# Transformer block with a second conditioned block: dense pieces placed otherwise over the steps of a turn, two score units taken a turn ahead

## The reference

```python
scale, shift = jnp.split(gelu(time_emb) @ Wt + bt, 2, axis=-1)
h = layer_norm(x, ln1_g, ln1_b) * (1.0 + scale[:, None, :]) + shift[:, None, :]
q, k, v = heads(h @ Wqkv)                       # 16 heads of 16
scores = einsum('bhqd,bhkd->bhqk', q, k) / 4 - torus_dist[:, None] * torus_scale[None, :, None, None]
scores = where(~mask[:, None, None, :], -1e30, scores)
x = x + merge(softmax(scores) @ v) @ Wout
h2 = layer_norm(x, ln2_g, ln2_b)
x = x + (gelu(h2 @ W1 + b1) @ W2 + b2)          # W1 256 x 1024
```

## Time and profile before

| | us |
|---|---|
| median of 3 runs | 1450.1 (1447.25 to 1451.61) |
| the profiled execution | 1447.55 |
| its span | 1445.7 |
| turn 0 | 85.8 |
| turns 1 to 7 | 107.3, 107.6, 107.6, 107.6, 108.7, 107.6, 107.9 |
| turns 8 to 15 with the end | 562.7 |

### The profile page before, as it was taken

The page is one execution under the profiler, slowest core; times in us unless marked ns, Lnnn a source line. Parts: engine busy times, 40 slices in busy tenths (PEclk is TensorE's granted clock), DMA queues, the critical chain, the costliest instruction groups (busy, mean ns, idle before and its releaser), DMA issues. The chain is left out here.

```text
span 1445.7 us, 24552 instructions
## 1 busy us (share of the span) xinstructions
PE 1310.9 (91%) x8789; PEld 1000.0 (69%) x8789; DVE 800.9 (55%) x2240; ACT 770.5 (53%) x1262; POOL 754.8 (52%) x939
## 2 busy tenths in 40 slices
PE   4898999999999999999999997889888888888887
PEld 3576777777777777777777776666666666665656
DVE  4766745746645645645644743474545646464452
ACT  3565764664665664665665662544545344454432
POOL 3788866876876875876876771020413223140323
PEclk9899999999999999999999999999999999999888
DMA  8432222222222222222223224443424242433100
GB/s 259 131 120 55 73 93 65 68 89 67 70 86 67 72 83 67 75 81 68 77 77 101 71 72 126 152 135 115 145 76 158 64 153 87 130 112 91 45 2 29
DMA packets 98259, 133.98 MB, mean 93 GB/s; under 512 B 16802, under 2 KB 51498, under 8 KB 98130
## 3 DMA queue, kind: packets, MB, share of 16 engines
q1 hardware_dynamic: 96850, 131.80, 30.4%
q10 hardware_dynamic: 1280, 0.53, 0.1%
HBM read 72.64 MB, written 58.75 MB: 91 GB/s over the span
## 5 line engine op out<-in xcount | busy, mean ns | idle before, releaser
L619 POOL TENSOR_SCALAR shifted<-shifted,row_max 128x512 f32<-128x512 f32 x512 | 358.9, 714 | 222.7 <-DVE row_max L1382 220.4
L1382 DVE CUSTOM_DVE_ANT_0 shifted<-score,bias 128x512 f32<-128x512 f32 x512 | 332.6, 687 | 255.9 <-PE score L857 163.6
L1093 ACT ACTIVATE probs<-turned 128x512 f32<-128x512 f32 x512 | 278.2, 596 | 211.5 <-PE turned L869 209.9
L869 PE MATMUL turned<-ident,shifted 128*128 128x128 f32 x2048 | 270.3, 275 | 6.8 <-POOL shifted L619 6.0
L869 PEld LDWEIGHTS turned<-ident,shifted 128*128 128x128 f32 x2048 | 233.8, 141 | 55.5 <-issue 26.4
L785 PE MATMUL dense<-w_down,hidden 128*128 128x256 f32 x1024 | 250.4, 381 | 0.8 <-ACT hidden L1074 0.8
L612 POOL TENSOR_SCALAR bias<-dist,scale 128x1024 f32<-128x1024 f32 x192 | 218.8, 1140 | 13.9 <-DMA down_bias<-in_L_cond_b 13.9
L857 PE MATMUL score<-k_rows,q_rows 97*128 97x512 f32 x512 | 205.1, 456 | 21.8 <-DVE row_max L1382 10.3
L785 PEld LDWEIGHTS dense<-w_down,hidden 128*128 128x128 f32 x1024 | 182.5, 190 | 32.5 <-issue 9.6
L765 PE MATMUL dense<-feat_m,w_up 128*128 128x512 f32 x768 | 188.9, 401 | 3.4 <-ACT hidden L1074 1.8
L765 PEld LDWEIGHTS dense<-feat_m,w_up 128*128 128x128 f32 x768 | 144.7, 192 | 37.2 <-ACT hidden L1074 5.2
(11 more groups left out here) (138 smaller groups left out, 1550.4 us busy)
## 6 DMA issues: line engine op xcount, KB each, us to landing
qk_rows<-qk_high SPq DMA_DIRECT2D x128, 256.0 KB
q_rows<-qk_rows SPq DMA_DIRECT2D x64, 384.0 KB
qk_rows<-qk_low SPq DMA_DIRECT2D x64, 256.0 KB
k_rows<-qk_rows SPq DMA_DIRECT2D x68, 192.0 KB
x_in_t<-in_x SPq DMA_DIRECT2D x8, 512.0 KB, 3.9
x_res<-in_x SPq DMA_DIRECT2D x8, 512.0 KB, 5.5
x_mid<-x_norm SPq DMA_DIRECT2D x8, 512.0 KB, 3.3
x_in_t<-x_mid SPq DMA_DIRECT2D x8, 512.0 KB, 3.9
```

The lines of the kernel that those rows point to most:

```text
L619: ins = pool.tensor_scalar(shifted[:, u % 3, i, :], shifted[:, u % 3, i, :], -1.0, row_max[:, t % 6:t % 6 + 1], ALU.mult, ALU.add)
L869: mm = pe.transpose(turned_bank[z % 2][:, HALF * kk + P * i:HALF * kk + P * i + P], shifted[:, u % 3, i, P * kt:P * kt + P], ident[:, :])
L1093: act.activation(probs[:, u % RING, 2 * pair:2 * pair + 2, :], turned_bank[z % 2][:, :].rearrange("p (a c) -> p a c", a=2), ACT.Exp)\
L1382: dve.tensor_tensor_reduce(shifted[:, u % 3, i, :], score_bank[t % 2], bias[:, u % 2, i, :], 1.0, 3.0e38, ALU.add, ALU.min, row_max[:, t % ...
```

## The change

The table `FIRST` puts the dense pieces elsewhere: `v` 2 and 3 a step apart at 3 and 4, `wout` 0 and 1 at 5 and 6 with `t1` behind them at 8 and 9, `qk` at 12, 13, 14 and 16 in place of 11 to 14, `up` two a step in steps 17, 18, 20 and 21 in place of four in 17 and four in 21, `down` from step 22 on in 14 parts in place of 11 from 25. The statistics and the normalization of the next input go from steps 2 and 4 to 4 and 6 (POOL's part from 2 to 4), the bias adds from 14 to 17 to 17, 18, 20 and 21. And the scores of units 0 and 1 of the next turn are taken by PE and DVE in steps 33 and 35 of this one (`AHEAD`), so that steps 0 and 1 of turns 1 to 7 hold none; turn 0 takes its own, turn 7 none ahead. POOL's and ACT's order for these units stays.

```diff
-    FIRST = {0: [("v", 0)], 1: [("v", 1)], 2: [("t3", 0), ("t3", 1)], 4: [("v", 2)], 5: [("v", 3), ("t1", 0)],
-             6: [("t1", 1)], 7: [("wout", 0)], 8: [("wout", 1)], 9: [("wout", 2)], 10: [("wout", 3)],
-             11: [("qk", 0)], 12: [("qk", 1)], 13: [("qk", 2)], 14: [("qk", 3)], 15: [("t2", 0), ("t2", 1)],
-             17: [("up", 0), ("up", 1), ("up", 2), ("up", 3)], 21: [("up", 4), ("up", 5), ("up", 6), ("up", 7)],
-             27: [("down", 0)], 30: [("down", 1)], 32: [("down", 2)], 35: [("down", 3)]}
+    FIRST = {0: [("v", 0)], 1: [("v", 1)], 2: [("t3", 0), ("t3", 1)], 3: [("v", 2)], 4: [("v", 3)],
+             5: [("wout", 0)], 6: [("wout", 1)], 8: [("t1", 0), ("wout", 2)], 9: [("t1", 1)], 10: [("wout", 3)],
+             12: [("qk", 0)], 13: [("qk", 1)], 14: [("qk", 2)], 15: [("t2", 0), ("t2", 1)],
+             16: [("qk", 3)], 17: [("up", 0), ("up", 1)], 18: [("up", 2), ("up", 3)], 20: [("up", 4), ("up", 5)],
+             21: [("up", 6), ("up", 7)],
+             25: [("down", 0)], 28: [("down", 1)], 31: [("down", 2)], 35: [("down", 3)]}
+
+    AHEAD = {33: 0, 35: 1}
     STEPS = UNITS + 5
-    FIRST_DOWN = {25: (0, 2), 26: (2, 5), 27: (5, 8), 28: (8, 12), 29: (12, 14), 30: (14, 17), 31: (17, 20),
-                  32: (20, 24), 33: (24, 26), 34: (26, 29), 35: (29, 32)}
-    FIRST_NORM = {2: ("stats", 0), 4: ("norm", 0), 11: ("stats", 1), 13: ("norm", 1)}
-    ADD_BIAS = {14: 0, 15: 1, 16: 2, 17: 3}
+    FIRST_DOWN = {22: (0, 2), 23: (2, 3), 24: (3, 6), 25: (6, 9), 26: (9, 12), 27: (12, 13), 28: (13, 16),
+                  29: (16, 19), 30: (19, 22), 31: (22, 24), 32: (24, 27), 33: (27, 28), 34: (28, 30), 35: (30, 32)}
+    FIRST_NORM = {4: ("stats", 0), 6: ("norm", 0), 11: ("stats", 1), 13: ("norm", 1)}
+    ADD_BIAS = {17: 0, 18: 1, 20: 2, 21: 3}
...
+    def begun(n, u):
+        return 0 < n < B and u in AHEAD.values()
...
-                        if k == 2 and n + 1 < B:
+                        if k == 4 and n + 1 < B:
                             inverse_std(n + 1, 0)
...
-                    if k < UNITS:
+                    if k < UNITS and not begun(n, k):
                         scores(n, k)
+                    if n + 1 < B and k in AHEAD:
+                        scores(n + 1, AHEAD[k])
...
-                    if k < UNITS:
+                    if k < UNITS and not begun(n, k):
                         shift_scores(n, k)
+                    if n + 1 < B and k in AHEAD:
+                        shift_scores(n + 1, AHEAD[k])
```

## The result

| | before | after |
|---|---|---|
| median of 4 runs each | 1448.67 (1446.25 to 1451.61) | 1426.82 (1425.15 to 1429.44) |
| profiled execution, its span | 1447.55, 1445.7 | 1427.12, 1425.3 |
| ahead of turn 0 | 43.5 (span less the rest) | 45.3 |
| turn 0 | 85.8 | 84.5 |
| turns 1 to 6 | 107.3, 107.6, 107.6, 107.6, 108.7, 107.6 | 104.4 each |

The account below looks back on a forecast made before the run. PE looks the bound, but waits drawn as busy lose 8.4 us a turn. Gains 1.2 + 1.5 + 0.2 - 0.4 = 2.5, taken as 2.3, times seven turns give 16 us: forecast 1433 us, range 1412 to 1450.

Parts of the forecast that it names:

- `qk` 3: Steps 15 to 17: moving it to step 16 gives ACT time to empty `t2`; 1.5 us a turn gained.
- the start: First `v` to step 8's pair: scores ahead cut lost time from 4.6 to 3.4 us, 1.2 gained.
- `up` two a step: Steps 17 to 22: 2.3 us of waits go, 2.1 paid back through ACT's table changes, 0.2 gained.
- `down` early: From step 22 in 14 parts: same products, five or six more changes of kind, -0.4 us a turn.
- the hand chain: Start of a turn, followed from the first `v`: shift 4 ends 9.1 us, shift 5 12.4.
- The wait named: Transposes after step 17's pair: 1.97 us later in place of 0.46, 1.5 lost, all of it to go.
- the gain of 2.3: Behind both blocks of `up` products: waits of 1.1 to 1.2 us a block go with two a step.
- Turn 0: First turn, without back work: what moves there cancels, 0 us, bounds -1 and +2.
- ACT as the bound: Rival, steps 17 to 22: added table changes cost PE 5.2 us; 1454 to 1462, decides from 4.4 lost; chance 0.12.
- the wait at unit 18: Transposes of unit 18 wait about 1.6 us for ACT's exps; forecast wrong if over 4 us.
- Nearly all waits go: Rival: start loses 1 us, not 3.4, and loads hide; 5 us and over a turn, 1405 to 1413; chance 0.12.
- Moved, not removed: Rival: normalization costs as much at step 6, ACT waits eat steps 15 to 17; 1444 to 1452; chance 0.14.

Follow-up runs that it names:

- experiment 3: The changed kernel with the next input's statistics and normalization back in steps 2 and 4: turn 105.67 us, median 1432.89, 0.9902 of before.
- experiment 4: The changed kernel with the four `qk` pieces back in steps 11 to 14, none in step 16: turn 105.06 us, median 1432.86, 0.9881 of before.
- experiment 8: The changed kernel with `down` back in 11 parts from step 25: turn 105.69 us, median 1430.43, 0.9882 of before.
- experiment 2: The kernel before with only the scores of two units taken ahead: most turns 106.55 us, median 1438.72, 0.9919 of before.

## Why the prediction was right, and where its steps were not

The sign, the place of the main waits and the total held: 1426.8 measured, 1433 forecast. That the total came within 0.9 us a turn is in part luck: of the four terms of the sum, `qk` 3 and `up` were put some 0.8 too high each, the start and `down` about 1.7 too low each by the single removals below, and these errors offset each other. What each part is worth to after, by taking it away alone, beside the forecast:

| part | forecast | taken away alone |
|---|---|---|
| scores ahead | together 1.2 | 1.64 (1.08 put in alone) |
| first norm at 6 | (in the 1.2) | 1.28 |
| `qk` 3 to step 16 | 1.5 | 0.67 |
| `up` two a step | 0.2 | -0.62 |
| `down` early, in 14 parts | -0.4 | 1.30 |
| bias adds | 0 | 0.0 |
| `v` 2 and 3 apart, `t1` and `wout` exchanged | (in the -0.4) | not run |
| sum | 2.5, taken as 2.3 | 4.27 |
| the turn | | 3.24 |

The parts do not add: taken away singly they make 1.0 more than together. Scores ahead are worth 1.08 without the rest and 1.64 with it. So part of the 1.0 lies between them and the rest, perhaps the norm, and some may lie between `up` and `down`; no run takes away just two of the parts.

**The start** (forecast 3.4 lost of 4.6). Right in kind: DVE is what the pairs wait for, and normalization in front of a shift costs a wait. A step that failed is the size of a pair of shifts: I took about 1.45, two lengths of 0.69 and a read each; by their starts they follow 0.61 apart, 1.22 to 1.3 a pair. In after shift 4 ends 8.55 us from the first `v` and shift 5 11.46, where the hand chain had 9.1 and 12.4; of the 0.9 by which it was late at shift 5 some 0.6 are the three pairs of shifts in it. Counted from start to start, pairs 4, 5, 6 and 8 lose 0.3, 0.4, 0.9 and 0.4, the transposes of unit 5 0.2, pair 11 0.5: 2.7. I also gave 1.1 to pair 8 behind the normalization, and it lost 0.4, because the attention of step 7 stands over it; experiment 3 shows what it costs without that cover. Pair 15 and the `qk` piece ahead of it, which lose 0.6 behind the second norm, I had not counted. Taken away alone, scores ahead and norm are worth 2.9 together, well over the 1.2 of the forecast; the singles overlap with other parts, so this is an upper mark.

**`qk` 3** (1.5). The wait named is gone, 0.53 in place of 1.97. The step that failed is the costing of the move as that alone: all four pieces shift, pair 15 then loses 0.5 behind the second norm and 0.3 is lost ahead of it, and experiment 4 shows 0.67 net.

**`up` two a step** (0.2). The payment was right in place and 0.6 too high: 2.1 forecast, 1.5 in the trace, 1.48 by taking the gelu away. The step that failed is the gain of 2.3. Nearly half of it (0.9 by the starts in before), the losses behind the second block, went through the early `down` products, whatever the grain of `up`. Against the 1.1 of the first block alone the change of grain loses. And the waits behind a block are not only DVE's and POOL's cold start, as the prediction had them: shift 19 stands idle 2.50 us in before for the bias that ACT makes late. The rule of the Trainium skill (ScalarE: Activation LUTs, Rules for kernel authors) to do all of one table set before switching is borne out here, by 0.62 us a turn. The drain that the same page adds to the load is not: ACT's rows have 1.29 from the start of a load to the gelu, and the next instruction of ACT starts within 0.02 of a load's end.

**`down` early** (-0.4). The step that failed outright: I counted it as the same products with more changes of kind, and it is the filler of steps 22 to 24, 1.30 won. The prediction said of this block that three pairs come close together, and did not ask what would then stand between them, nor that ACT's bias for unit 23 comes late there. It has POOL (2.2 a step) as what the steps must cover; in experiment 8 pair 24 waits behind ACT's bias.

**Turn 0** (0, bounds -1 and +2): 1.2 less by one profile of each, which shows no gain. Before without gelu has the same work in turn 0, and its profile gives 83.9 where that of before gives 85.8; the granted clock over it is 0.98 and 0.96.

**The rivals.** ACT as the bound: it is full from 489.4 to 500.5, but the wait at unit 18 is 1.0, far under the 4.4 from which that rival decides. Nearly all waits go: no, some 5 us a turn are left. Moved, not removed: true of the step from before's `up` waits to after's table waits, not of the turn. Of the marks that I set, the turn was to be 105 to 105.5 and is 104.4; the eight loads, POOL's 3.65 (under 5), the clean transposes of unit 15 and the 0.5 at the first `down` product are there; the wait at unit 18 is 1.0 and not 1.6. Pairs 5 to 8 with their transposes lose 1.9, inside the 1 to 5 that I set, and the first scores ahead wait for no load: the pair at 540.85 needs 0.66 to its successor, like those around it.

## What to carry to other kernels

A light step of the first engine lays bare whatever another engine is late with. Here the bias that ACT makes behind the gelus came 3.3 us late for DVE in both kernels, and cost PE nothing where `down` products stood in those steps; moving them there was worth 1.30 us a turn. So look for the steps where a helper is late, and put filler there. Put a long instruction of a queue that others wait for behind the longest piece of work that can cover it, and cost each piece that a move takes away from under another. Undo each part alone once a bundle has won: here one part of it lost, and leaving that out, with the norms, `t1`, `wout` and `qk` placed anew, brought 10 to 13 us more.

## What the runs showed of the hardware that was not expected

**A change of tables costs its load alone, and starts early.** In after the gelus of 490.71 end about 492.10, the load runs from 492.11 to 493.39 and the exps start at 493.41. Nor does the load wait for the operand of the ACTIVATE behind it: that at 489.42 began while PE, which had started the two `up` pieces at 488.36 (3.01 for both), could not have ended the first before about 489.8. The Trainium skill (ScalarE: Activation LUTs, What ACT_TABLE_LOAD costs) gives the same 1283 ns for the load; no row here shows the drain that it adds. A group of turn 4 of after:

```profile
L1083 ACT ACT_TABLE_LOAD x4 | 5.1, 1283 | 0.1
```

**The same DVE instruction takes half as long again beside POOL.** The second norm in before, with POOL idle for most of it, POOL first:

```profile
491.00 1.37 POOL L619 TENSOR_SCALAR shifted<-shifted,row_max 128x512 f32<-128x512 f32 x2 [2.32 <-DVE row_max L1382]
...
488.35 1.44 DVE L1222 TENSOR_SCALAR x_norm<-x_res,mean_var,rstd 128x256 f32<-128x256 f32 x4
```

and in after, with POOL at work through most of it:

```profile
475.18 1.12 POOL L619 TENSOR_SCALAR bias<-dist,scale 128x1024 f32<-128x1024 f32 x1
476.27 1.43 POOL L626 TENSOR_SCALAR shifted<-shifted,row_max 128x512 f32<-128x512 f32 x2
...
475.88 2.29 DVE L1231 TENSOR_SCALAR x_norm<-x_res,mean_var,rstd 128x256 f32<-128x256 f32 x4
```

1.44 us against 2.29 for the same four. By an estimate from these rows this is why pair 15 waits in after: with the 0.85 less on DVE, shift 14 (478.59 to 479.88) would have ended before that pair's start at 479.33. That it is a port which both engines use was not tested by itself. The Trainium skill (SBUF — State Buffer, section Who interferes with whom) tells of a port pair that one of DVE and POOL takes for a whole instruction while the other blocks, and names DVE's `tensor_scalar` among the operations that can take it; whether this one did, no row shows.

**Odd turns.** In a few profiles single turns are 1 to 2.7 us longer than their neighbours with the same work. Three of the four (108.2 twice in experiment 2, 110.05 in before without gelu) hold one stretch of 3.4 us in which the granted clock fell from its level of 2.4 to that of 1.2 GHz, with PE busy through it. That can make 1.7 at most, so it covers the 1.6 of experiment 2 and not the 2.7 of the other. The fourth, 108.7 in before, is at full clock. What made the clock fall, and what the rest is, no run explains.
